# Two of nine taps sampled densely, with hats in half sets made a key tile ahead

## What is computed

```
attn = softmax(einsum('bhqd,bhkd->bhqk', q, k) * scale)
x = proj(einsum('bhqk,bhkd->bhqd', attn, v)) + x
offset_feat = conv2d(concatenate([x, feat_s * 2]), W_off, pad=0)
om = conv2d(offset_feat, W_om, pad=1) + b_om          # offsets and masks, 8 groups x 9 taps
val = sum over 4 corners of gather(feat_s, corner) * bilinear weight
out = relu(einsum('bgckhw,ogck->bohw', val * sigmoid(mask), W_dcn) + b_dcn) + x
```

## Time and profile before

| | before |
|---|---|
| median of 3 runs | 12,792.7 us (12,789.01 to 12,793.89) |
| profiled execution | 12,790.43 us, span 12,788.6 us |
| mean granted TensorE clock | 0.819 |
| busy: TensorE matmul, VectorE, ScalarE, GpSimd | 70%, 62%, 23%, 84% of the span |

### The profile page before, as it was taken

How to read it: one execution, slowest core, us unless ns; L and a number is a source line. 1 busy time by engine, 2 the same in 40 slices (tenths; PEclk the granted TensorE clock), 3 DMA queues, 4 the chain that set the end, 5 groups by cost and what they waited for, 6 DMA issues and landing times. The chain is left out here.

```text
span 12788.6 us, 126443 instructions
## 1 busy us (share of the span) xinstructions
PE 8894.0 (70%) x34036; PEld 3273.8 (26%) x34036; DVE 7910.4 (62%) x9169; ACT 2914.1 (23%) x3357; POOL 10703.5 (84%) x24581
## 2 busy tenths in 40 slices
PE   5666778765777767777666777766687766778732
PEld 1222222222222222222222222222232222222211
DVE  3466666666666666656666656666566666656633
ACT  2222222211222211222122222211222221222200
POOL 0488888887888888888788888888788888888888
PEclk8888888887888887888788888878788887888865
DMA  3222211112111111111211111111211111111111
GB/s 94 75 65 67 78 29 25 28 29 61 29 32 28 28 28 29 29 29 31 54 35 29 29 27 27 28 28 29 62 24 34 29 28 29 29 29 25 28 24 23
DMA packets 458806, 469.41 MB, mean 37 GB/s; under 512 B 150432, under 2 KB 274464, under 8 KB 458016
## 3 DMA queue, kind: packets, MB, share of 16 engines
q0 software_dynamic: 262144, 268.96, 10.3%
q1 hardware_dynamic: 97952, 119.95, 3.5%
q10 hardware_dynamic: 97920, 71.35, 1.8%
HBM read 390.46 MB, written 69.21 MB: 36 GB/s over the span
## 5 line engine op out<-in xcount | busy, mean ns | idle before, releaser
L408 POOL DMA_INDIRECT g<-patches,idx x8192 | 7862.1, 960 | 1254.6 <-issue 1180.1
L404 POOL TENSOR_TENSOR carrier<-carrier 128x1 f32<-128x1 f32 x15872 | 2766.3, 203 | 140.1
L982 DVE TENSOR_TENSOR ring<-ring,hats 128x1024 f32<-128x1024 f32 x1024 | 1259.3, 1230 | 2520.4 <-PE ring L655 2187.3
L494 ACT ACTIVATE p<-ring 128x1024 f32<-128x1024 f32 x2048 | 2089.2, 1022 | 2812.3 <-PE ring L622 1936.6
L597 PE MATMUL ring<-k,q 128*128 128x512 bf16 x4096 | 1763.9, 529 | 1216.2 <-DVE mx L844 796.3
L844 DVE TENSOR_REDUCE mx<-ring 128x1 f32<-128x1024 f32 x2048 | 2381.1, 1218 | 300.9 <-PE ring L597 300.9
L621 PE MATMUL ring<-q,k 128*128 128x512 bf16 x4096 | 1598.3, 390 | 307.3 <-ACT p L494 84.0
L622 PE MATMUL ring<-q,k 67*128 67x512 bf16 x4096 | 1584.9, 387 | 0.0
L655 PE MATMUL ring<-fx,hats 64*128 64x512 f32 x4096 | 1203.2, 666 | 230.8 <-ACT hats L482 178.8
L984 DVE TENSOR_REDUCE dval<-ring 128x16 f32<-128x1024 f32 x1024 | 1254.1, 1225 | 35.4
L678 PE MATMUL ps_a<-p,v 128*64 128x512 f32 x4096 | 1110.9, 621 | 2.0 <-ACT p L494 2.0
(11 more groups left out here) (117 smaller groups left out, 5707.2 us busy)
## 6 DMA issues: line engine op xcount, KB each, us to landing
g<-patches,idx POOLq DMA_INDIRECT x8192
patch_in<-in_fpad ACTq DMA_DIRECT2D x544, 64.0 KB
patches<-patch_out ACTq DMA_DIRECT2D x136, 256.0 KB
k<-k_parts SPq DMA_DIRECT2D x96, 256.0 KB
q<-q_parts SPq DMA_DIRECT2D x192, 128.0 KB
k_parts<-v SPq DMA_DIRECT2D x16, 768.0 KB
q_parts<-p SPq DMA_DIRECT2D x32, 384.0 KB, 2.6
p<-in_x SPq DMA_DIRECT2D x4, 2048.0 KB
```

Of the source, the lines that this page charges most:

```text
L404: last = nc.gpsimd.tensor_tensor(carrier[:, col:col + 1], carrier[:, 0:1], carrier[:, 0:1], ALU.add)
L408: nc.gpsimd.indirect_dma_start(out=g[:, part, j - CUTS[part] * GROUPS, :], out_offset=None, in_=patches[b], in_offset=bass.IndirectOffsetO ...
L494: nc.scalar.activation(p[:, n % 4, :, :], ring[u % 2][:, :, :], ACT.Exp, scale=SCALE)\
L982: then(V.tensor_tensor(cells, cells, hy[:, at * HEIGHT:(at + 1) * HEIGHT].unsqueeze(2).to_broadcast([128, HEIGHT, GC]), ALU.mult))
```

## The change

`DENSE` goes from 1 to 2: seven taps are gathered (56 gathers a tile, the last part has 8), two are sampled densely (16 groups a tile, two in each key tile). The hats of a tile are made in four half sets of four groups. A half set takes one slot of `ring` (x distances in its first half, y distances in the second) where a whole set took two, and goes into one of two buffers in turn. It is made in the key tile before its first use, the first of a step ahead of the maxima's rows. The use numbers follow: `hats_at` says at which key tile a half set is made, `dense_use` places the two columns of a key tile behind its two score pairs. `g` loses the gap between its parts, and `fs_s` now lies in the first hat buffer.

```diff
-DENSE = 1
+DENSE = 2
...
+SETS = 2 * DENSE
+SET_GROUPS = GROUPS // 2
+SET_TILES = KT_TILE // SETS
+SET_COLS = SET_GROUPS * (128 + HEIGHT)
...
-        g = sb("g", [128, PARTS, 2 * GROUPS, PATCH])
+        g = sb("g", [128, PICKS, PATCH])
...
-        hats = sb("hats", [128, DENSE * GROUPS * (128 + HEIGHT)])
-        hx = hats[:, 0:DENSE * GROUPS * 128]
-        hy = hats[:, DENSE * GROUPS * 128:]
-        fs_s = hats[:, 0:QB]
+        hats = sb("hats", [128, 2, SET_COLS])
+        hx = [hats[:, i, 0:SET_GROUPS * 128] for i in range(2)]
+        hy = [hats[:, i, SET_GROUPS * 128:SET_COLS] for i in range(2)]
+        fs_s = hx[0]
...
+        def hats_at(s, kt):
+
+            t, j = divmod(kt + 1, KT_TILE)
+            return ((t, j // SET_TILES),) if t in dense_tiles(s) and j % SET_TILES == 0 else ()
...
+        def set_and_place(j, k):
+
+            return j // SET_TILES, j % SET_TILES * DENSE + k
+
+        def dense_use(s, t, j, k):
+            kt = t * KT_TILE + j
...
+            return first_use(s, kt) + len(hats_at(s, kt)) + 1 + 2 * k
...
+            def make_hats(s, b, t, i):
+                k = hat_use(s, t, i)
+                wait_slot_full(act, before_att(s, b, k), k)
+                nc.scalar.activation(hx[i % 2], ring[k % 2][:, 0, :], ACT.Abs, bias=plus_x, scale=-1.0)
+                nc.scalar.activation(hy[i % 2], ring[k % 2][:, 1, 0:SET_GROUPS * HEIGHT], ACT.Abs).then_inc(ring_free[k % 2], 1)
+                wait_slot_read(act, before_att(s, b, k), k)
+                nc.scalar.activation(hats[:, i % 2, :], hats[:, i % 2, :], ACT.Relu, bias=ones_s[:, 0:1], scale=-1.0)\
+                    .then_inc(hats_ready, 1)
...
+            def distances(s, b, t, i):
...
+                for j in range(SET_GROUPS):
+                    mm(ring[k % 2][:, 0, j * 128:(j + 1) * 128], dpos[:, t, 1, at + j:at + j + 1].to_broadcast([128, 128]),
+                       ident_s[:, :], start=True, stop=True)
...
+                if place == 0:
+                    pe.wait_ge(hats_ready, tile_number(s - 1, t) * SETS + i + 1)
...
-                if dense and j == 0:
-                    distances(s, b, t)
+                for hat in hats_at(s, kt):
+                    distances(s, b, *hat)
                 for pair in range(2):
                     scores_of_pair(s, b, kt, pair)
                     if dense and pair < DENSE:
...
+                    if 0 in dense_tiles(s):
+                        distances(s, b, 0, 0)
                     max_to_rows(s, b)
                     scores(s, b, 0, fresh)
...
-                for d in range(DENSE):
-                    k = dense_use(s, t, j, d)
-                    then = InOrder(dve, dve_dense, (n * GROUPS + j) * DENSE + d)
+                for part in range(DENSE):
+                    k = dense_use(s, t, j, part)
+                    i, place = set_and_place(j, part)
+                    then = InOrder(dve, dve_dense, (n * KT_TILE + j) * DENSE + part)
```

More of the change, by code:

```diff
@@ L224, in before_om, with max_use @@
             return halves_before(s) + uses_in(s) // 2 + b * (USES_KV // 2) + USES_KV // 2 + s * (USES_OM // 2) + k // 2
-        def first_use(s, kt):
-            dense, (t, j) = dense_tiles(s), divmod(kt, KT_TILE)
-            behind = USE_D * sum(d < t for d in dense) + (t in dense) * (2 * DENSE * (j > 0) + DENSE * j)
+        def hats_at(s, kt):
+            t, j = divmod(kt + 1, KT_TILE)
+            return ((t, j // SET_TILES),) if t in dense_tiles(s) and j % SET_TILES == 0 else ()
+        def max_use(s, k):
+            return USE_Q + USE_MAX + (0 in dense_tiles(s)) + k
@@ L230, in first_use, with last_step_use, hat_use @@
+        def first_use(s, kt):
+            dense = dense_tiles(s)
+            behind = sum(2 + (k // KT_TILE in dense) * DENSE + len(hats_at(s, k)) for k in range(kt))
+            return max_use(s, USE_M) + behind
+        def last_step_use(s, t, i):
+            return (s - STEPS) + dense_tiles(s).index(t) * USE_D + i * (1 + SET_GROUPS)
+        def hat_use(s, t, i):
             if isinstance(s, int) and s >= STEPS:
-                return (s - STEPS) + behind
-            return USE_Q + USE_MAX + USE_M + 2 * kt + behind
@@ L234, in hat_use @@
-        def hat_use(s, t, d, axis):
-            return first_use(s, t * KT_TILE) + 2 * d + axis
+                return last_step_use(s, t, i)
+            kt = t * KT_TILE + i * SET_TILES - 1
+            return first_use(s, kt) if kt >= 0 else USE_Q + USE_MAX
         def score_use(s, kt, pair):
[L238 to L244, removed]
+            dense = kt // KT_TILE in dense_tiles(s)
@@ L246, in part_number @@
+            return first_use(s, kt) + len(hats_at(s, kt)) + (2 * pair if dense else pair)
+        def set_and_place(j, k):
+            return j // SET_TILES, j % SET_TILES * DENSE + k
+        def dense_use(s, t, j, k):
+            kt = t * KT_TILE + j
+            if isinstance(s, int) and s >= STEPS:
+                i, place = set_and_place(j, k)
+                return last_step_use(s, t, i) + 1 + place
+            return first_use(s, kt) + len(hats_at(s, kt)) + 1 + 2 * k
         def part_number(s, t, part):
@@ L408, in gather @@
                         nc.gpsimd.indirect_dma_start(
-                            out=g[:, part, j - CUTS[part] * GROUPS, :], out_offset=None, in_=patches[b],
+                            out=g[:, j, :], out_offset=None, in_=patches[b],
                             in_offset=bass.IndirectOffsetOnAxis(ap=idx[:, t, j:j + 1], axis=0),
@@ L535, in step @@
                     for t in dense_tiles(s):
[L536 removed]
+                        for i in range(SETS):
+                            make_hats(s, b, t, i)
                         for part in range(PARTS):
@@ new lines, in columns_of_group @@
+            def columns_of_group(s, b, t, j, part, fresh):
+                k = dense_use(s, t, j, part)
+                wait_slot_free(pe, before_att(s, b, k), k)
+                i, place = set_and_place(j, part)
+                group = i % 2 * SET_GROUPS + place
+                if place == 0:
+                    pe.wait_ge(hats_ready, tile_number(s - 1, t) * SETS + i + 1)
+                    if fresh and t == 1 and i == 0:
+                        pe.wait_ge(fx_loaded, b * 32 + 32)
+                for half in range(2):
+                    rows = slice(half * WIDTH, (half + 1) * WIDTH)
+                    last = mm(ring[k % 2][:, half, :].rearrange("p (y c) -> p y c", c=GC), hx[i % 2][rows, place * 128:(place + 1) * 128],
+                              fx[rows, :, group * GC:(group + 1) * GC], start=True, stop=True)
```

98 lines of the change are left out of this document (35 added, 63 removed).

## The result

| | before | after |
|---|---|---|
| median | 12,793.0 us (4 runs, 12,789.0 to 12,793.9) | 15,782.3 us (4 runs, 15,770.8 to 15,810.2) |
| profiled execution | as above | 15,810.2 us, span 15,808.4 us |
| mean granted TensorE clock | 0.819 | 0.834 |

A forecast was written before the change was run, and what follows sets the result against it. The prediction took GpSimd's gathers, closely followed by a PSUM-slot chain, to bound the kernel, and that chain after the change. 846.5 + 30 x 491.5 + 216 + 412 + 12 gave 16,230 us, 27% slower; range 15,600 to 17,200 (80%).

The forecast's parts named there:

- The bound moves off GpSimd: Whole changed kernel: GpSimd waits for `val` in every step, busy near 9,400 us, 58%.
- the two near-equal bounds: Step before the change: GpSimd 376.5 us, the other three engines 359.7; fewer gathers gain at most some 500 us.
- Both columns in one slot: Key tile of the changed kernel: the second column product cannot be written while VectorE reads the first; 4.12 us each.
- The second bound is a chain, not an engine: Key tile before: 5.08 us from 1.17 filling, 2.94 VectorE passes with hand-over and 0.97 scores, through two PSUM slots.
- A key tile of 8.24 us: Key tile of the changed kernel: two turns of 4.12 us through one slot, against 5.08 before.
- just hidden: From second columns to the next key tile's first: TensorE's own 3.90 us fits within the turn's 4.12.
- Hats, 1.75: Key tiles that make a half set: 5.87 us against 4.12, so 1.75 more, 15 times a step, 26 us.
- Parts and clock, 21 + 12 us: Key-tile phase of a step: sampling parts between dense groups add 21 us, time at 1.2 GHz adds 12.
- the 302.7: First to last columns of a step at the full clock: 31 x 8.24 + 21 + 26 = 302.7 us.
- the 15% of the prediction: Key-tile phase: TensorE's clock is at 1.2 GHz for 15% of it, 12 us a step.
- the rival's 19,130 us: Clock stays low: TensorE bounds at 11.1 us a key tile, 588 us a step; above 17,200 us got 10%.
- The step: 491.5 us forecast: Each of steps 2 to 31 takes 491.5 us; three image preparations add 72 each, 216 in all.

The follow-up runs named there:

- Experiment 2: The changed kernel with three adds on `carrier` ahead of each gather in place of two: 15,861.6 us, ratio 1.2368.
- Experiment 1: The kernel before with 56 gathers a tile, its last picked tap left out, and one dense tap as before: 12,338.0 us, ratio 0.9625.
- Experiments 3 and 4: The changed kernel without VectorE's y-hat multiply for one dense group of each key tile: the first group's in 3 (14,452.1 us), the second's in 4 (15,488.9 us).
- experiment 6: The changed kernel with both score pairs of a key tile ahead of both columns, which then stand in different slots: 14,329.7 us, ratio 1.1206.
- Experiment 8: The kernel before with 56 gathers a tile and one dense tap, VectorE's y-hat multiply left out as well: 12,247.1 us, ratio 0.9572.
- experiment 5: The changed kernel with `weigh` of the key tile before moved on TensorE from behind the second column product to ahead of it: 15,163.0 us, ratio 1.1856.
- The first: The changed kernel with one dense tap (half sets kept) and one add ahead of each gather in place of two: 12,304.2 us, ratio 0.9622.
- the two slower neighbours: The kernel before with one add a gather, 16,391.8 us; and one dense tap, half sets, one add, with `weigh` ahead of the second score pair, 16,467.1 us.
- the repeat: One dense tap, half sets and one add ahead of each gather, run once more unchanged on another chip: 16,227.8 us, ratio 1.2699.

## Why the prediction was right, and where its terms were off

- **The bound moves off GpSimd: right, shown.** Experiment 2 gave it 1,010 us more work, and the kernel grew by the tail's 37 us. The forecast of its page line (9,400 us, 58%) came out as 9,342 and 59%.
- **What the gathers could bring: right.** Experiment 1 gives 482 us, below the 500 that the two near-equal bounds allowed.
- **Both columns in one slot: right, shown.** Experiments 3 and 4 part place from load, and experiment 6, which changes the slots and one piece of order, takes back 1,453 us of 2,990, with what the clock gave back in it.
- **"The second bound is a chain, not an engine": wrong for the plain key tile of before.** Experiment 8 left it at 5.08 us. The 0.45 us between VectorE's reduce and the scores at 6306.05 in the earlier trace rows, read as the hand-over, was `weigh`, still running on TensorE from 6304.18 on:

```profile
6305.09 1.03 PE L678 MATMUL ps_b<-p,v 128*64 128x512 f32 x4
...
6306.05 0.39 PE L621 MATMUL ring<-q,k 128*128 128x512 bf16 x1
```

- **A key tile of 8.24 us: the term mis-sized by this.** The hand-over measures 0.06 us. The turn is then 3.72 and not 4.12, and the other interval is the 3.90 of TensorE's work that the prediction had called "just hidden" and which now sets it: 7.62. Over 31 intervals that is 19 us a step less.
- **Hats, 1.75: too small.** The interval was worked out as 5.87 and measured 6.00 at the full clock, but it stands against 3.90 and not 4.12: 2.1 each, 31.5 us in place of 26.
- **Parts and clock, 21 + 12 us: the sum right, the split roughly.** From the first multiply of the first key tile of step 20 to that of the last are 302.8 us; less 236.2 and 31.5 leaves 35. An estimate from the intervals gives the parts 18 of it: five with a part's passes took 5.52 to 5.98 against 3.72, five with its turns 4.66 or 4.77 against 3.90, and six with turns and a half set some 0.8 over 6.00 (by the shortest such ones in experiment 4's kernel, 6.67 and 6.89). The clock is left with 17. That the whole came out at the 302.7 that was forecast for the full clock is luck: 31 key tiles were 19 us too long in the forecast, and the clock and the hats make up for it.
- **The clock: as assumed.** The phase's granted clock of 0.93 is 2.4 GHz for all but about 15% of it (1.2 GHz there), the 15% of the prediction. The rule of the Trainium skill, "TensorE: Matmul & The Clock Gate", section "A second HAM failure mode: psum-queue depth-cycling", is borne out in direction by this trace (0.99 before, without the gap of 1.41 us). Here the swing is worth some 17 us a step by the estimate above; the rival's 19,130 us did not come.
- **The step: 491.5 us forecast, 478.6 found.** From the start of step 2 to that of step 31 are 14,080.4 us; the 26 steps without a preparation average 478.6, and the three with one take 201 us more in all, where 216 were summed. Those 13 us times 29, 374 us, are most of the difference of 423 between the summed and the profiled time. Another 26 are step 1, where the change added 66 us and not 95: 24 key tiles by 2.54 in place of 3.16 explain 15 of the 29, the rest I did not follow. From the start of step 31 to the end are 908 us where 915.5 were summed.

So the mechanism stood, and the error of 2.8% comes in the main from one reading: time for which an engine was held by its own work was called a hand-over.

## What to carry to other kernels

Busy times that fit under the bound say nothing about work that shares a buffer in strict turn: write down which slot each use takes and what stands between two uses of one slot. Before an interval is called a hand-over, look at what the engine that takes over was doing in it, and at how long the same hand-over is where nothing else runs. When such a turn is the bound, change which slot the uses fall into (experiment 6, 1,453 us) before filling the gap with other work (experiment 5, 620 us), and compare the granted clock too, for a gap that closes can give some of it back; and when a version is faster in one session, repeat it in another.

## What the runs showed of the hardware, not expected

- TensorE can start 0.06 us after VectorE's last instruction on the slot ends; the other way, from the start of columns to VectorE's start, takes 1.17 us, of which the products are 1.06.
- With gathers 1.33 us apart the same kernel ran in 12,304 us once and 16,228 another time; with 1.47 us no run in any session was disturbed, the kernel before among them in the same sessions (12,790.8 to 12,819.6 us). The first ran on one chip, the two slower neighbours on a second, the repeat on a third. In the kernel before with one add, all distances of a tile were written by 9958.83 and ScalarE started on them at 9966.64:

```profile
9957.81 1.02 PE L641 MATMUL ring<-ident_s,minus_x 128*128 128x512 f32 x2
...
9966.64 1.11 ACT L474 ACTIVATE hats<-ring,base_s 128x1024 f32<-128x1024 f32 x1 [29.34 <-remote]
```

In that trace VectorE's multiply waits 238 times for "remote" (2,837 us in all, up to 37.0) and `exp` 369 times (1,844 us, up to 12.2); the trace of the kernel before has no such wait. The adds, by their number or by the spacing that they give, decide together with something that differs between the sessions, the chip perhaps. A spacing between 1.33 and 1.47, or the same kernel on each of the three chips, was not tried. The adds look like ballast and are not: with one add the same program cannot be relied on.
